# Expert products in pairs and a state copy moved from ScalarE to VectorE in a fused scan kernel

## The reference

```python
# selective scan; layer 0: 4 directions, 384 channels; layer 1 (mamba block): 1 direction, 768 channels
dA = exp(dt[..., None] * A)                 # 16 states per channel
h  = h * dA + (dt * u)[..., None] * B_t     # along 1024 positions
y  = sum over the 16 states of h * C_t
# experts of layer 1: 4 experts, 384 -> 1536 -> 384
h = gelu(einsum('bsd,edh->ebsh', x, w1) + b1)
y = einsum('ebsh,ehd->ebsd', h, w2) + b2
out = einsum('bse,ebsd->bsd', masked_top2_probs, y)
```

## Time and profile before

| what | value |
|---|---|
| median of 3 runs | 6451.98 us |
| profiled execution, its own time | 6456.0 us |
| its span | 6454.2 us |
| TensorE busy | 5405.0 us (84%) |
| VectorE busy | 4830.5 us (75%) |
| ScalarE busy | 3408.2 us (53%) |
| GpSimd busy | 4086.9 us (63%) |
| mean granted clock of TensorE | 0.931 of full speed |

### The profile page before, as it was taken

How to read it: one execution, slowest core, us unless ns; L and a number is a source line. 1 busy time by engine, 2 the same in 40 slices (tenths; PEclk the granted TensorE clock), 3 DMA queues, 4 the chain that set the end, 5 groups by cost and what they waited for, 6 DMA issues and landing times. The chain is left out here.

```text
span 6454.2 us, 59474 instructions
## 1 busy us (share of the span) xinstructions
PE 5405.0 (84%) x16384; PEld 3093.5 (48%) x16384; DVE 4830.5 (75%) x5044; ACT 3408.2 (53%) x5402; POOL 4086.9 (63%) x3001
## 2 busy tenths in 40 slices
PE   6776777779999878878999977886999997788899
PEld 2222232245555444435555535443555554444677
DVE  7999679758888758856878776794788886677554
ACT  3433444356666546636666654553766664554322
POOL 6999459547777627826778743781777772676121
PEclk8889888889999989989999989998999998899999
DMA  5555134246666424616676623551666760553110
GB/s 192 207 209 209 58 128 168 87 144 241 219 240 225 156 82 171 203 48 221 218 241 222 240 83 133 187 173 65 223 243 214 248 212 31 186 192 115 52 44 32
DMA packets 339295, 1059.06 MB, mean 164 GB/s; under 512 B 31331, under 2 KB 121443, under 8 KB 333833
## 3 DMA queue, kind: packets, MB, share of 16 engines
q1 hardware_dynamic: 338952, 1055.17, 47.1%
HBM read 1046.13 MB, written 8.91 MB: 163 GB/s over the span
## 5 line engine op out<-in xcount | busy, mean ns | idle before, releaser
L810 PE MATMUL banks<-prod,ident 128*128 128x512 f32 x2640 | 1466.1, 649 | 556.5 <-DVE prod L1014 429.4
L963 POOL TENSOR_TENSOR h<-half_du_a,Bb 128x512 f32<-128x512 f32 x768 | 967.7, 1277 | 107.1 <-DVE banks L1005 56.1
L810 PEld LDWEIGHTS banks<-prod,ident 128*128 128x128 f32 x2640 | 475.8, 197 | 1101.1 <-DVE prod L1014 774.2
L905 ACT ACTIVATE banks<-half_delta_a,A 128x512 f32<-128x512 f32 x1152 | 781.8, 686 | 397.5 <-DVE prod L1014 302.3
L1005 DVE TENSOR_TENSOR_SCAN banks<-banks,h 128x512 f32<-128x512 f32 x660 | 806.7, 1222 | 170.2 <-ACT banks L905 97.3
L972 POOL TENSOR_TENSOR h<-h,half_C_a 128x512 f32<-128x512 f32 x360 | 460.8, 1280 | 367.6 <-ACT half_carry_a L891 256.4
L810 PE MATMUL banks<-h,ident 128*128 128x512 f32 x1200 | 653.3, 628 | 3.0 <-POOL h L972 3.0
L1014 DVE TENSOR_TENSOR prod<-banks,half_C_a 128x512 f32<-128x512 f32 x792 | 548.0, 692 | 126.7 <-DMA half_C_a<-half_rows 17.3
L834 PE MATMUL banks<-Cb,w_a 128*128 128x256 f32 x2304 | 568.0, 386 | 0.0
L1005 DVE TENSOR_TENSOR_SCAN banks<-banks,half_carry_a,h 128x512 f32<-128x512 f32 x396 | 506.6, 1279 | 57.6 <-ACT banks L905 37.9
L403 PE MATMUL banks<-prod,ident 128*128 128x512 f32 x648 | 375.8, 720 | 196.9 <-DVE prod L545 152.1
(11 more groups left out here) (325 smaller groups left out, 10289.6 us busy)
## 6 DMA issues: line engine op xcount, KB each, us to landing
Bb<-half_rows SPq DMA_DIRECT2D x640, 512.0 KB, 4.0
Cb<-half_rows SPq DMA_DIRECT2D x320, 512.0 KB, 4.2
w_a<-w_in SPq DMA_DIRECT2D x256, 576.0 KB, 5.4
half_C_a<-half_rows SPq DMA_DIRECT2D x160, 512.0 KB, 6.7
w_b<-w_in SPq DMA_DIRECT2D x128, 576.0 KB, 5.2
Bb<-rows SPq DMA_DIRECT2D x96, 512.0 KB, 4.2
Cb<-rows SPq DMA_DIRECT2D x96, 512.0 KB, 3.9
half_C_b<-half_rows SPq DMA_DIRECT2D x80, 512.0 KB, 6.8
```

What stands on the lines that cost most here:

```text
L810: eng.matmul(ps[:, 0, :], m.ident[:, :], src, start=n == 0, stop=added(s) == (i + 1) * N, skip_group_check=True).then_inc(st.summed, 1)
L905: eng.activation(slot(s), m.delta[:, i % 2, :], ACT.Exp, scale=x.A(j, n)).then_inc(st.decay, 1)
L963: eng.tensor_tensor(m.dBu[:, s % DRIVES, :], m.du[:, i % 2, :], m.B[b % BRING][:, cols(s % 2)], ALU.mult).then_inc(st.dbu, 1)
```

## The change

There are four edits, all in `fused_scans`.

- Both products up of a pair are issued at step 0, and both products down at step 7.
- `evict` moves from step 9 to step 10, with `accumulate` two steps behind it, and the list runs one step longer.
- ScalarE keeps only the states of VectorE's steps. The states of GpSimd's steps in a first half are copied by VectorE, after the next step's scan and before that step's product.
- These copies have a semaphore of their own, `kept_held`. GpSimd's `weigh` waits for it, and so does the scan of a GpSimd step in a second half.

```diff
     def kept(s):
         block = TILES * N
-        full, at = s // (2 * block), s % (2 * block)
-        return full * block + min(at, block)
+        full, at = s // (2 * block), min(s % (2 * block), block)
+        both = full * block + at
+        theirs = full * TILES * LANE_POOL + pooled(at)
+        return both - theirs, theirs
+
+    def last_state(s, src):
+        at = 0 if reverse(s) else HALF - 1
+        return src[:, at:at + 1]
...
     def up_from(s):
-        return [2 * starts[s - r] + r for r in range(2) if s - r in starts]
+        return [2 * starts[s], 2 * starts[s] + 1] if s in starts else []
...
     def down_from(s):
-        return [2 * starts[s - 6 - r] + r for r in range(2) if s - 6 - r in starts]
+        return [2 * starts[s - 7], 2 * starts[s - 7] + 1] if s - 7 in starts else []
...
     def evict_from(s):
-        return [(starts[s - 9] + 1) * 2 // PER - 1] if s - 9 in starts and (starts[s - 9] + 1) * 2 % PER == 0 else []
+        return [(starts[s - 10] + 1) * 2 // PER - 1] if s - 10 in starts and (starts[s - 10] + 1) * 2 % PER == 0 else []
...
 # ScalarE
             def keep(s):
-                last = 0 if reverse(s) else HALF - 1
-                src = held[pooled(s) % HELD] if by_pool(s) else slot(s)
-                if by_pool(s):
-                    eng.wait_ge(st.scanned, s + 1)
-                else:
-                    eng.wait_ge(st.prod, own(s) + 1)
-                eng.activation(carry(s), src[:, last:last + 1], ACT.Copy).then_inc(st.kept, 1)
+                eng.wait_ge(st.prod, own(s) + 1)
+                eng.activation(carry(s), last_state(s, slot(s)), ACT.Copy).then_inc(st.kept, 1)
...
-                if SLOTS <= s < STEPS + SLOTS and first_half(s - SLOTS):
+                if SLOTS <= s < STEPS + SLOTS and first_half(s - SLOTS) and not by_pool(s - SLOTS):
                     keep(s - SLOTS)
...
 # GpSimd, weigh
                 eng.wait_ge(st.scanned, s + 1)
                 if first_half(s):
-                    eng.wait_ge(st.kept, kept(s + 1))
+                    eng.wait_ge(st.kept_held, kept(s + 1)[1])
...
 # VectorE
+            def keep(s):
+                eng.wait_ge(st.scanned, s + 1)
+                eng.tensor_copy(carry(s), last_state(s, held[pooled(s) % HELD])).then_inc(st.kept_held, 1)
...
                 if s < STEPS:
                     scan(s)
+                    if by_pool(s - 1) and first_half(s - 1):
+                        keep(s - 1)
                     if not by_pool(s):
                         weigh(s)
```

More of the change, by code:

```diff
@@ L660, in down_from @@
     def down_from(s):
-        return [2 * starts[s - 6 - r] + r for r in range(2) if s - 6 - r in starts]
+        return [2 * starts[s - 7], 2 * starts[s - 7] + 1] if s - 7 in starts else []
     def evict_from(s):
-        return [(starts[s - 9] + 1) * 2 // PER - 1] if s - 9 in starts and (starts[s - 9] + 1) * 2 % PER == 0 else []
-    LAST = max(STEPS, pair_at(UNITS // 2 - 1) + 12)
+        return [(starts[s - 10] + 1) * 2 // PER - 1] if s - 10 in starts and (starts[s - 10] + 1) * 2 % PER == 0 else []
+    LAST = max(STEPS, pair_at(UNITS // 2 - 1) + 13)
     def chunk(k):
@@ L902, in decay @@
                         if first_half(s - SLOTS):
-                            eng.wait_ge(st.kept, kept(s - SLOTS + 1))
+                            eng.wait_ge(st.kept, kept(s - SLOTS + 1)[0])
                 x, j, _ = lane(i)
@@ L998, in scan @@
                 if not first_half(s):
-                    eng.wait_ge(st.kept, kept(s) - TILES * N + s % (TILES * N) + 1)
+                    mine, theirs = kept(s - TILES * N + 1)
+                    if by_pool(s):
+                        eng.wait_ge(st.kept_held, theirs)
+                    else:
+                        eng.wait_ge(st.kept, mine)
                     initial = carry(s)
@@ L1719, in build @@
         s_fused = stage("fused", "projected", "ones", "low", "stored", "dt", "magnitude", "exped", "logged", "delta", "du",
-                        "turned", "kept", "decay", "dbu", "scanned", "prod", "pooled", "summed", "taken",
+                        "turned", "kept", "kept_held", "decay", "dbu", "scanned", "prod", "pooled", "summed", "taken",
                         "hidden", "gelu", "down", "evicted", "accumulated", "sent", "reloaded", "ahead",
```

## The result

The changed kernel takes 6271.75 us (median; 6265.91 to 6282.0), against 6449.48 us for the kernel before. The ratio is 0.9725 with a 95% interval of 0.9708 to 0.9741. The prediction was 6352 us with a range down to 6290 us: the sign was right, and the gain of 178 us is nearly twice the 102 us of the sum. The profiled execution took 6282.0 us, with a span of 6280.2 us.

A forecast was written before the change was run, and what follows sets the result against it. VectorE paces mamba without guests, TensorE nearly bounds the scans, and engines wait for one another in mamba with guests. Gains of 78 (mamba) and 54 (scans) less 18 (loop) and 12 (bursts) give 102 us: 6352 us, range 6290 to 6450.

The forecast's parts named there:

- the evict was costed at nothing: Evict one step later: same two steps to the next expert's first product down, one more behind the last; 0 us.
- its rule for such stalls: Scans of layer 0: VectorE's stalls cost time only where TensorE has caught up with it.
- The scans' gain: Scans of layer 0: copy and products up fill TensorE's 66.5 us idle time; 18 us a stage, between 0 and 56.
- lose 26: Mamba stage with guests: 22 us from the copy leaving ScalarE plus 4 us from both products up in one go.
- the bursts: Mamba, pairs seven steps apart: two ups and two downs fall in one step, delaying the next add; 4 us a stage.
- the loop: GpSimd's product waits for the next scan and VectorE's copy: 5.3 us against 5.16 a round; 18 us lost in all.
- The cover I named, the product ring: Mamba: a ring of three products, over 8 us of VectorE's steps, covers the 5.2 us burst of four units.
- One sign that the prediction named against itself: VectorE's products (L1014) waiting for TensorE's add (L810) would prove the prediction wrong.
- ScalarE's waits for them would fall under 10 us: Scans stage: ScalarE's wait for the products up falls from 36.6 us to under 10.
- That VectorE's copy waits for GpSimd: Rival: each of 300 copies waits for GpSimd's running operation, 0.8 us each; 6500 us, chance 0.11.
- TensorE as the bound of the scans altogether: Rival: in the scans TensorE's gaps only move and only mamba gains, 48 us; 6404 us, chance 0.18.
- The rival in which the stalls go entirely: Rival: the scans give 40 us each in place of 18, since ScalarE's waits are short; 6286 us, chance 0.10.

The follow-up runs named there:

- e9: Kernel before with one edit, evict at step 10 in place of 9: 6377.80 us, ratio 0.9892.
- e6: Changed kernel with evict back at step 9 in place of 10: 6343.58 us, ratio 0.9829 to the kernel before.
- e2: Kernel before with the copy edit alone, VectorE copying the states of GpSimd's steps: 6377.41 us, ratio 0.9898.
- e14: Kernel before with the last of three channel tiles of every product up left out: 6346.91 us, ratio 0.9843.
- e1: Kernel before with one edit, both products up of a pair at step 0: 6387.10 us, ratio 0.9907.
- e4: Kernel before with both products up at step 0, both down at step 7, evict at 10, ScalarE copying all states: 6343.59 us, ratio 0.9841.
- e5: Changed kernel with products down at steps 6 and 7 and evict at 9: 6330.34 us, ratio 0.9811 to the kernel before.
- e7: Changed kernel with both products down at step 6 in place of 7, evict at 10: 6264.65 us, ratio 0.9714 to the kernel before.
- e3: Kernel before with one edit, both products down at step 7, evict staying at step 9: 6517.80 us, ratio 1.0111.
- e11: Changed kernel, but ScalarE copies all states in the mamba stage without guests: 6273.42 us, ratio 0.9726 to the kernel before.
- e8: Changed kernel with VectorE's copy straight behind the scan it copies from, ahead of the next scan: 6274.80 us, ratio 0.9723 to the kernel before.
- e15: Changed kernel with the last of three channel tiles of every product up left out: 6178.44 us, ratio 0.9582 to the kernel before.

## Why the prediction was wrong in size

**Where it failed: the evict was costed at nothing.** The prediction said of the evict that it "keeps its distance to the next expert's first product down" and took no gain for the step behind the last one. e9 measures 20 us for each scans stage and 72 us in all, e6 the same from the other side. The stand was in the trace of before, 28.3 us for a scans stage, and the prediction doesn't name it; its rule for such stalls was that they "are felt only where TensorE has caught up with it". The timeline at 3424.82 shows TensorE catching up within a microsecond and then idle for 2.47.

**The term that rested on the busy share.** The scans' gain was a third of TensorE's idle time, 18 us a stage. It measured 40 us: 20 from the evict (e9) and 15 to 19 from the copy (e2). TensorE's idle time fell from 66.5 to 38.6 us, and its busy time fell too, from 781.3 to 766.9 us, with the granted clock going from 0.98 to 0.99. So 14 of the stage's 42 us came out of time that the prediction took as fixed when it said that both edits can only fill TensorE's idle time. e14 shows what the 92% was worth as a bound: the first halves hardly noticed lighter work, the second halves did. The copy's gain lies in the first halves, where GpSimd is released as described and TensorE holds little down.

**Mamba: the sum was right, its parts less so.** A stage with guests was to lose 26 less 4 for the bursts and 3.6 for the loop, 18 us; the three lost 17.4 us in the mean. That agreement is luck. The copy alone brings 11 us (e2), not 22 less its loop, and the products up alone 11 us (e1), not 4. The two overlap: the units with the evict, without the copy, bring 15 us in the mean (e4), and the copy adds 2 to that. The first half fell to 205 us, near the forecast 200; the second stayed at 191, where e1, e4, e5 and e7 have 187 or 186. It is not the copy: e5 and e7 have it, and e9 has not and stands at 191.9. The granted clock of that half was 0.95 in the changed kernel and in e9 and 0.96 to 0.98 in e1, e4 and e5, but 0.95 in e7 as well. Why it did not fall stays open.

**Both products down.** The prediction took nothing for them in the scans, which e3 bears out, and 4 us a mamba stage for the burst. Next to the products up in one go they cost 4 to 7 us there (e6 against e5, with the evict at 9), so the size was about right; alone they cost 23 us (e3). The cover I named, the product ring, was not the point of e3; what stands between two products up counted there, at least for a part. One sign that the prediction named against itself did appear, products of VectorE that wait for TensorE's add. Over the whole kernel, before and changed:

```profile
DVE prod L1014 <- PE banks L810: 3.1, 4, 1.0
DVE prod L1023 <- PE banks L816: 13.8, 12, 4.3
```

Of the 13.8 us 12.3 lie in the three mamba stages with guests, 1 to 6 us a stage, two stands of 4.3 us among them: the ring's cover does give way at times.

**The products up.** That ScalarE's waits for them would fall under 10 us in a scans stage was right (9.1 us in the second stage, though 11.7 and 10.6 us in the other two). Such a wait stood before 32 gelus of the stage and now stands before 15. What it brought there alone was 7 to 10 us (e1). In the mamba first half the waits of the earlier trace rows are 2.0 us each, longer than the 1.46 us of a unit, and they fell from 11.9 to 4.7 us only.

**VectorE's copy and GpSimd's loop.** The copy is hidden behind its scan, as taken, and the loop of 5.3 us measured 5.28. Its price in the half without guests was 7.2 us where 24 rounds of 0.15 gave 3.6; e11, which keeps ScalarE's copies there, gives 6.5 of it back. Why it is twice the price of the rounds stays open.

**The rivals.** That VectorE's copy waits for GpSimd did not happen: no copy took over 151 ns, though 46 of the 300 lie wholly inside a running operation of GpSimd. The wide casts of the earlier trace rows are another matter: 12 of the 96 took 1.00 to 2.71 us, and all 12 began while an operation of GpSimd ran; none of the 84 short ones did. By the rule of the Trainium skill's SBUF — State Buffer (Who interferes with whom), a copy or cast from SBUF to SBUF can take the port pair shared with GpSimd. The casts agree with it, and the copies of one column show no such hold. The trace of the changed kernel has a copy at 3889.11 of 0.15 us, in the middle of one of GpSimd's drives:

```profile
3888.26 1.27 POOL L964 TENSOR_TENSOR h<-half_du_a,Bb 128x512 f32<-128x512 f32 x1
3889.11 0.15 DVE L1015 COPY half_carry_a<-h 128x1 f32<-128x1 f32 x1
```

TensorE as the bound of the scans altogether is refuted by e9, which took no work from it and gained 20 us a stage; e14 leaves it a share in the second halves. The rival in which the stalls go entirely was the nearest: it put 40 us on each scans stage and gave 6286 us, and it had 0.10. Its price came out by luck, since its reason (ScalarE's short waits) is a small part of it.

## What to carry to other kernels

A busy share of 92% does not say how far an engine is the bound: with that share lighter work came back at 30% in one kind of half and at 70% in the other. Take a stand of another engine that feeds it, find it in the timeline, and look whether the busy engine goes idle a microsecond later; if so, the stand costs time. Here 56 us less of it went with 60 us less in the three stages. And busy time is not fixed: it fell by 14 us in a stage with the same products. When an operation waits for the end of a chain, as an evict does, count the steps between the two and try one more before anything else. And an edit can be harmful alone and nearly harmless with its partner, so price an order by what comes between two things that a third engine waits for together.

## What the runs showed of the hardware

- VectorE copied one fp32 column from SBUF to SBUF in 142 to 151 ns (changed kernel, 300 copies), over twice the 59 ns of a one-column memset, and did not wait for a GpSimd operation in progress (46 of them lie inside one). A cast of 512 columns took 0.41 to 0.43 us without one and 1.00 to 2.71 us when one was running (kernel before).
- A copy that does not depend on the scan before it fits between the scan and the product that does: 1.36 us with it, 1.35 without (changed kernel). Ahead of an independent scan the same copy cost 0.2 us (e8).
- With 288 of 2580 matmuls left out of a scans stage, TensorE's granted clock fell from 0.98 to 0.97 (e14) and from 0.99 to 0.98 (e15).
